# Dealing the ratio pieces of a batch anew over its attention phase and its shared expert

## What is computed

```python
def cond(r, k, v, w, u, time_emb):       # k = v = fside, one column per channel
    decay = exp(-exp(w)) * (0.5 + 0.5 * tf)
    ek  = exp(minimum(k, 30)); ekv = ek * v
    a, b = forward scans   a = a*decay + ekv,  b = b*decay + ek   # nf, df
    c, d = the same scans backwards                               # nb, db
    euk = exp(minimum(u + k, 30))
    num = nf + nb - ekv + euk * v;  den = df + db - ek + euk
    return sigmoid(r) * (num / maximum(den, 1e-8)) * (0.8 + 0.2 * tf)

x = x + gla_attention(cond(x, ..., L0_cond_w, L0_cond_u))    # gated linear attention, layernorm, Wo
x = x + moe(cond(x, ..., L0_cond2_w, L0_cond2_u))            # shared expert + 6 of 16 experts
x = x + ssd(cond(x, ..., L1_cond_w, ...))                    # second layer
x = x + mxfp8_ffn(cond(x, ..., L1_cond2_w, ...))
```

## Time and profile before

| what | value |
|---|---|
| median of 3 runs | 3940.6 us (3938.12 to 3940.74) |
| the profiled execution's own time | 3943.84 us |
| its span, first to last instruction | 3942.0 us |
| mean granted TensorE clock | 0.917 |
| PE busy, DVE busy, ACT busy, POOL busy | 3380.4, 2652.5, 1180.4, 502.9 us |

### The profile page before, as it was taken

How to read it: one execution, slowest core, us unless ns; L and a number is a source line. 1 busy time by engine, 2 the same in 40 slices (tenths; PEclk the granted TensorE clock), 3 DMA queues, 4 the chain that set the end, 5 groups by cost and what they waited for, 6 DMA issues and landing times.

```text
span 3942.0 us, 36808 instructions
## 1 busy us (share of the span) xinstructions
PE 3380.4 (86%) x12493; PEld 2058.3 (52%) x12493; DVE 2652.5 (67%) x3769; ACT 1180.4 (30%) x1948; POOL 502.9 (13%) x404
## 2 busy tenths in 40 slices
PE   1877877877878999999999778898889888988898
PEld 0553653643555777677777435543454346434643
DVE  6877778788785777888888254664566455645563
ACT  1332332332331445334334122212221223123310
POOL 1002002002003111111111112020212011201100
PEclk9888988988989999999999887899889988998799
DMA  3201211211203778787877510132013201220011
GB/s 137 81 24 43 80 34 38 84 34 35 76 23 115 251 246 273 228 275 241 267 269 250 218 53 33 75 112 86 32 75 112 86 32 75 92 106 32 7 58 43
DMA packets 276635, 436.66 MB, mean 111 GB/s; under 512 B 52320, under 2 KB 189536, under 8 KB 263904
## 3 DMA queue, kind: packets, MB, share of 16 engines
q1 hardware_dynamic: 256768, 379.85, 28.5%
q0 software_dynamic: 19680, 54.46, 4.4%
HBM read 364.59 MB, written 93.77 MB: 116 GB/s over the span
## 4 chain that ended last, share of the span: by engine, by line
PE 59%; DVE 24%; DVEq 6%; ACT 5%; issue 3%; DMA 1%; POOL 1%; SPq 0%; ACTq 0%; POOLq 0%
PE bank L1019 11%; PE bank L1048 6%; PE bank L1287 6%; PE bank L1300 4%; PE bank L1308 4%; PE bank L835 3%; PE bank L1216 3%; PE bank L1156 3%; DVE sb_gla L1888 3%; PE bank L1194 2%; DVE sb_ratio L1863 2%; DVEq L1869 2%; PE bank L1025 2%; PE bank L815 2%; PE bank L1252 2%
## 5 line engine op out<-in xcount | busy, mean ns | idle before, releaser
L1019 PE MATMUL bank<-sb_xT,sb_work 128*128 128x256 f32 x2304 | 512.6, 382 | 1.6 <-issue 0.8
L1019 PEld LDWEIGHTS bank<-sb_xT,sb_work 128*128 128x128 f32 x2304 | 438.9, 192 | 75.1 <-issue 17.5
L835 PE MATMUL bank<-sb_gla,sb_work 128*128 128x256 f32 x896 | 261.1, 444 | 111.8 <-DVE sb_work L1890 99.2
L1048 PE MATMUL bank<-sb_work,sb_hT 128*128 128x512 f32 (+1 forms) x666 | 296.1, 592 | 0.0
L835 PEld LDWEIGHTS bank<-sb_gla,sb_work 128*128 128x128 f32 x896 | 189.6, 219 | 174.8 <-DVE sb_work L1890 120.1
L815 PE MATMUL bank<-sb_hT,sb_work 128*128 128x512 f32 x384 | 182.1, 622 | 99.0 <-DVE sb_hT L1837 99.0
L1300 PE MATMUL bank<-sb_parts,sb_gla 128*128 128x512 f32 x512 | 238.8, 610 | 4.5 <-ACT sb_gla L1632 4.1
L1308 PE MATMUL bank<-sb_parts,sb_gla 128*128 128x512 f32 x512 | 230.8, 593 | 6.3 <-DVE sb_work L2469 6.3
L1287 PE MATMUL bank<-sb_work,sb_parts 128*128 128x512 f32 x512 | 231.7, 612 | 2.7 <-ACT sb_work L1645 2.7
L1888 DVE TENSOR_TENSOR sb_gla<-sb_gla,sb_work 128x1024 f32<-128x1024 f32 x112 | 145.9, 1303 | 129.9 <-PE bank L835 124.4
L1156 PE MATMUL bank<-sb_parts,sb_hT 128*128 128x512 f32 x512 | 231.1, 611 | 0.0
(11 more groups left out here) (403 smaller groups left out, 5950.2 us busy)
## 6 DMA issues: line engine op xcount, KB each, us to landing
sb_work<-scratch_gu SPq DMA_DIRECT2D x63, 1408.0 KB
sb_parts<-scratch_mx SPq DMA_DIRECT2D x16, 3072.0 KB, 11.3
sb_work<-moe_w SPq DMA_DIRECT2D x63, 512.0 KB, 6.4
scratch_y<-sb_work SPq DMA_DIRECT2D x48, 512.0 KB, 7.4
sb_parts<-scratch_fq SPq DMA_DIRECT2D x24, 1024.0 KB, 8.0
sb_work<-w_qkvg SPq DMA_DIRECT2D x64, 256.0 KB, 2.4
scratch_gu<-moe_w SPq DMA_DIRECT2D x32, 512.0 KB, 5.8
sb_parts<-fT SPq DMA_DIRECT2D x48, 256.0 KB
```

The source lines that it names most:

```text
L835: mm = pe.matmul(dst.rearrange("p (h n l) -> p h n l", h=HPC, l=size), kS[u % 2][:, k * P:(k + 1) * P], late[:, :, k, :, 1, :], start=True ...
L1019: mm = pe.matmul(dst, egu[j % 3][:, which * NC + k, m * P:(m + 1) * P], xt[j % 2][:, k, :], start=(k == 0), stop=(k == NC - 1))
L1048: mm = pe.matmul(bank(YB[s]), einter[j % 2][0:n, a:a + P], edn[j % 3][0:n, m * D:(m + 1) * D], start=(m == 0), stop=(m == EC - 1))
```

## The change

The same pieces run in the same order with the same operands. Their places differ:

- pieces 0 to 5 (a whole column) run at the front of a batch, before level 0;
- the levels hold pieces 6 to 10 (c = 0), 11 to 14 (c = 1), 15 to 17 (c = 2), 18 and 19 (c = 3);
- 20 to 23 stay; 24 and 25 run after the layer norm's reciprocal, 26 to 28 after the gating with ratio 1, 29 after the shared expert's first product;
- the shared expert's steps 1 to 5 hold 4, 2, 4, 4 and 4 pieces (30 to 47);
- `gate0` of the next batch is split: three columns after piece 41, the last at the end;
- the two picks leave `route` and stand after the first product (in all batches);
- ACT's `exps` and SP's `load_f` follow.

```diff
+        LEVEL_PIECES = (range(6, 11), range(11, 15), range(15, 18), range(18, 20))
+        SHARED_PIECES = (range(29, 30), range(30, 34), range(34, 36), range(36, 40), range(40, 44), range(44, 48))
+        SHARED_EXPS = {1: 1, 3: 2, 4: 3, 5: 4}
...
                     lay_out(b * NC + c - 1)
-                    if c >= 2:
-                        load_f(2 * NC * b + NC + c)
-                load_f(2 * NC * (b + 1) + 1)
+                    load_f(2 * NC * b + NC + c + 1)
...
                 spread(b * NC)
+                exps(2 * NC * b + NC + 1)
                 for c in range(NC):
                     u = b * NC + c
                     if c:
                         carry_over(u - 1)
-                    if c == 1:
-                        exps(2 * NC * b + NC + c)
                     if c + 1 < NC:
                         for i in range(3):
                             evacuate(u + 1, i)
-                            if c == 2 and i == 0:
-                                exps(2 * NC * b + NC + c)
+                            if (c, i) in ((1, 0), (2, 2)):
+                                exps(2 * NC * b + NC + c + 1)
...
-                    if c == 3:
-                        exps(2 * NC * b + NC + c)
...
                 act.activation(sdv, bank(6), ACT.Sqrt, bias=eps_ln).then_inc(ln_sd.sem, 1)
+                if b + 1 < NB:
+                    exps(2 * NC * (b + 1))
                 for c in range(NC):
                     act.wait_ge(x1a.sem, x1a.at(b, c + 1))
                     act.activation(ch(h1, c), ch(X1[b % 2], c), ACT.Sigmoid).then_inc(sig1.sem, 1)
-                if b + 1 < NB:
-                    exps(2 * NC * (b + 1))
...
-                    for n in range(4 * j, 4 * j + 4):
-                        if n % 6 == 5 and b + 1 < NB:
-                            exps(2 * NC * (b + 1) + n // 6 + 1)
+                    if j in SHARED_EXPS and b + 1 < NB:
+                        exps(2 * NC * (b + 1) + SHARED_EXPS[j])
...
                 r0 = 6 * (2 * NC * b + NC)
+                for n in range(6):
+                    ratio_piece(r0 + n)
...
-                        if i < 5:
-                            ratio_piece(r0 + 5 * c + i)
+                        if i < len(LEVEL_PIECES[c]):
+                            ratio_piece(r0 + LEVEL_PIECES[c][i])
...
                 dve.reciprocal(sdv, sdv)
                 dve.drain()
+                if b + 1 < NB:
+                    for n in (24, 25):
+                        ratio_piece(r0 + n)
...
                 q.then_inc(h1_ready.sem, 1)
+                if b + 1 < NB:
+                    for n in (26, 27, 28):
+                        ratio_piece(r0 + n)
...
                     tt(inter[j % 2], sgt[j % 2], bank(5), ALU.mult).then_inc(m_prod.sem, 1)
+                    if j == 0:
+                        if not last:
+                            ratio_piece(6 * (2 * NC * b + NC) + SHARED_PIECES[0][0])
+                        picks(b)
...
-                    if not last:
-                        for n in range(4 * j, 4 * j + 4):
-                            ratio_piece(12 * NC * (b + 1) + n)
+                    if not last and j:
+                        for n in SHARED_PIECES[j]:
+                            ratio_piece(6 * (2 * NC * b + NC) + n)
+                            if n == 41:
+                                gate0(b + 1, range(NC - 1))
                 if not last:
-                    gate0(b + 1)
+                    gate0(b + 1, range(NC - 1, NC))
```

13 lines of the change are left out of this document (9 added, 4 removed).

## The result

The changed kernel takes **3912.5 us** (median of four runs, 3908.3 to 3916.8) against 3939.8 for the kernel before: a ratio of 0.9926, with a 95% interval of 0.9912 to 0.9940. It is 27 us faster; 50 were forecast, and the time lies 2.5 us above the range. The profiled executions differ by more than the medians, 3943.84 against 3908.90, since the one of before was 4.0 us over its median and the one of after 3.6 under.

A forecast was written before the change was run, and what follows sets the result against it. DVE was taken as the limit in two places, idle in three. Shared expert -39, levels -12, output 3 x 0.2 gave -50.4 on 3943.84: 3893.4, less 3.2 for the profiled execution, 3890 us; range 3875 to 3910.

The forecast's parts named there:

- Front: Start of each of four batches: a whole column of 14.4 us fits into 18.72 us of DVE idle time, cost nothing.
- Rival B: Front: POOL's first product is blocked until DVE's column ends, 1.9 us x 4 = 8, time 3898; chance 0.07.
- Levels: Levels of four batches: +1 for c = 2 and -4 for c = 3, -3 a batch, -12 in all.
- c = 2 costs 1.3 at most: Levels of c = 2: p3 in place of p0 adds 1.30 us up to level 2, then PE sets the pace; taken as +1.
- The 4 us taken for c = 3: Levels of c = 3: fewer pieces at levels 0 to 2 save 3.8 to 4.5 us a batch, taken as 4.
- keeps its length: Level 3 of c = 3: it already waited 0.72 us for PE at its end, so its 4.97 us stay.
- Output: Output of three batches: two pieces, 3.77 us, in a hole of 3.65 before the first addition, +0.2 each.
- Routing and shared expert: Routing to next gating, three batches: 13.5 us less by the count, taken as 13 a batch, -39 in all.
- the walk: Batch 1's routing and shared expert, event by event: gating ends at 667.3 instead of 680.83, 13.5 us less.
- rival D: Shared expert: PE drops to its lower clock, 144 matmuls at 0.87 us instead of 0.44, time about 4045; chance 0.03.
- Rival C: Shared expert: a silu behind a waiting exponential stalls PE once a batch, 3 x 4.5 = 13, time 3903; chance 0.07.
- In the last batch only the picks move: nothing: Last batch's routing: the picks move past one product and the same table work follows, cost 0.

The follow-up runs named there:

- the levels alone: The kernel before with only the changed front column and level pieces, its shared expert, routing, picks, gating and output pieces kept: 3939.8 us, ratio 0.9970.
- products held back: The changed kernel with POOL's two products for columns 2 and 3 held until DVE's level 3 products of the column before are done: 3899.6 us, ratio 0.9864.
- the kernel with one piece moved: The changed kernel with five pieces in column 1's levels and two in column 2's, ACT's exponentials there moved ahead of the third evacuation: 3888.4 us, ratio 0.9853.

## Why the forecast was too high

**Front: right.** 0 forecast; +0.6, +0.6 and -0.1 us measured. POOL's products did meet piece 5 there (0.75 became 1.04 to 1.49), inside the 4.1 us that were left. Rival B's mechanism is real, but not at the front.

**Levels: the sum nearly right, its terms not.** -12 forecast, -9.4 in the profiles, -11.8 for the part alone. The step "c = 2 costs 1.3 at most" failed: it measured +3.0 to +3.6. I had counted the pieces alone. With the exponentials behind the third evacuation, POOL's product started right after it, onto level 2's L1889 (+1.06). PE then waited longer and worked at a lower clock behind level 3 (0.81), which is the other 1.2 us. A wait of this length doesn't always cost the clock: in the levels alone the scores of level 2 took 1.99 us after 2.98 us of waiting, and those of level 3 3.78 after 2.77. The experiments on this column bear the collision out: products held back give 3.8 us there, and the column with a piece less and without the two stretches is 7.4 shorter. The 4 us taken for c = 3 measured 5.4 in batch 1 and 8.0 in batch 0, which covered the miss by luck. Levels 0 to 2 came as forecast (5.73, 6.61 and 5.27 us against 5.7, 6.6 and 5.2). The step that level 3 "keeps its length" failed: it took 3.64 us instead of 4.97.

**Output: nearly right.** +0.2 forecast, +0.2, +0.2 and +0.5 measured.

**Routing and shared expert: the failed step.** -13 a batch forecast; -9.5, -8.5 and -12.0 measured. The order of events was right to 0.5 us at every product where PE ran at its full clock, and in the one batch with neither the memset's collision nor the slow start the gating ended at the 81.8 of the walk. The step that failed is the walk's price of the instructions: it took each at its length in the kernel before, and added nothing for who runs beside it or for PE's clock at its start. Two terms were missing. First, the maximum against the memset, 2.44 us in two of three batches. In the kernel before the memset ran beside scans and a product at no cost, so its row gave no warning; I had priced every piece alone and never asked what POOL would be doing at its new time. Second, the first 32 matmuls at 15.85 us instead of the 14.00 of the earlier trace rows, 1.5 to 1.9 us a batch. In the kernel before, the low clock of this place was over by then; here it reached into them. This is the low clock of rival D, for some 4 matmuls instead of 144, but not by D's mechanism: the clock is low before these matmuls begin, and the slow start goes with the changed levels more than with the new order. Why the levels shift it stays open. Rival C, the stall between ACT and PE, did not occur: the longest wait of PE within the stage is under 2 us.

**Last batch: wrong.** "In the last batch only the picks move: nothing" cost 2.2 us by the first index write and 2.8 by the first expert tile. I had followed the picks on DVE but not the chain behind `place`, which alone decides when the expert stage begins. The other 2.8 of the 5.6 us came between the first index write and the tile; they differ by 2 to 3 us between kernels with the same order there too (82.4 and 84.7 in the two profiles of before), so the change isn't shown to cause them.

**The rest** of the way to the median is no cause in the program: 3.2 us that I took off for the execution of before, and 3.6 by which the execution of after lies under its median.

The Trainium skill, page "SBUF — State Buffer", section "Who interferes with whom", says that a VectorE instruction with two SBUF inputs contends with a GpSimd instruction that reads SBUF but not with one that only writes it, and that `tensor_scalar` can contend with either in its two-port mode. The traces agree in these cases: product against product 0.42 to 1.48, scan beside the memset unstretched, predicated copy with a PSUM input beside a product unstretched, TENSOR_SCALAR beside the memset 0.43 to 2.87. I had used that section for its lock alone and missed the half on which instruction meets which. The same section lets whoever issues first keep the port. The rows don't show that: here the maximum starts at 646.04 and the memset at 646.80, and the maximum was the one stretched; in batch 0 of the kernel with one piece moved the memset's row starts first (351.57 against 352.10). In both the maximum ends 0.29 us after the memset, at 648.91 and 353.68. The starts of POOL's rows are rough, so the rule isn't refuted either.

## What to carry to other kernels

A moved instruction has to be priced at its new time together with what the other engine of the pair does then. What holds the matmul engine up can cost twice if the matmul clock falls with it: 3.4 us of work taken out of column 2 gave 7.4, of which 2.8 came where TensorE only computed, at a higher clock. Look for the waits of the helper engine level by level before choosing places; the pieces put where VectorE waited cost next to nothing, and moving one of them, with its exponentials, was worth 19 to 24 us where the whole change was worth 27 to 37. Where a stage hands over through many small writes, follow their chain from its first link, and keep them away from the load of weights that the next stage waits for.

## What the runs showed of the chip that I had not expected

- Small indirect writes can go with slow large loads: with five of them beside the weight loads, 256 KB landed in 12.7 us (median), and in 5.5 in the kernel that differs only in the memset's place and has none there. It isn't a fixed price: one batch later four writes ran beside the same loads, which landed in 4.3 us.
- After a memset and a drain put between indirect writes, GpSimd began its next write 10.22 us later, about as long as such a write takes to land (11.9); the eight other such places (three batches of three kernels) had 6.74 to 11.09. That the drain waits for the landings is the likely reading, not shown.
- The same program runs its batches in several lengths: 296.2 to 301.5 us in the kernel before, 283.8 to 288.4 in the changed one. For the changed one's batch 2 (283.8 and 288.4), 2.4 of the 4.6 us are the maximum meeting the memset or not, and some 2 are the next front at a lower clock. And the routed experts, the same code in all kernels here, took from 2673.2 to 2685.5 us in sixteen profiles. A gain below 5 us is better read from a stretch of the trace than from a time.
